# Turning the q and k rows of a second attention layer: DVE blocks and SBUF transfers in place of TensorE transpositions

## What is computed

```python
q = rmsnorm((x @ Wq + bq).reshape(b, n, 32, 128), gq)
k = rmsnorm((x @ Wk + bk).reshape(b, n, 32, 128), gk)
v = (x @ Wv + bv).reshape(b, n, 32, 128)
attn = softmax(einsum("bnhd,bmhd->bhnm", q, k) / sqrt(128))
out = einsum("bhnm,bmhd->bnhd", attn, v).reshape(b, n, 4096) @ Wo + bo
```

## Time and profile before

| | us |
|---|---|
| median of the runs shown | 2192.4 |
| span of the profiled execution | 2194.5 |
| PE busy in it | 2089.6 (95%) |
| DVE busy | 1678.1 (76%) |
| ACT busy | 1349.4 (61%) |
| POOL busy | 1216.8 (55%) |

### The profile page before, as it was taken

The page is one execution under the profiler, slowest core; times in us unless marked ns, Lnnn a source line. Parts: engine busy times, 40 slices in busy tenths (PEclk is TensorE's granted clock), DMA queues, the critical chain, the costliest instruction groups (busy, mean ns, idle before and its releaser), DMA issues. The chain is left out here.

```text
span 2194.5 us, 37916 instructions
## 1 busy us (share of the span) xinstructions
PE 2089.6 (95%) x10535; PEld 1756.7 (80%) x10535; DVE 1678.1 (76%) x2972; ACT 1349.4 (61%) x3637; POOL 1216.8 (55%) x985
## 2 busy tenths in 40 slices
PE   6999999999999778999999999999999999878998
PEld 4788888888888657888888888888888888756786
DVE  6788888888888876878888788888878888875422
ACT  5877777777776455656666565666656565544321
POOL 3878777787786554546454554545445463354300
PEclk9999999999999989999999999999999999979999
DMA  2534344434344422444444444434444343533210
GB/s 83 136 100 126 108 110 113 114 105 125 104 117 130 134 62 71 116 108 116 116 109 99 121 107 115 109 100 117 114 112 112 99 116 92 131 104 105 87 53 25
DMA packets 165887, 231.69 MB, mean 106 GB/s; under 512 B 47280, under 2 KB 77136, under 8 KB 165744
## 3 DMA queue, kind: packets, MB, share of 16 engines
q1 hardware_dynamic: 165744, 229.97, 39.4%
HBM read 114.23 MB, written 6.55 MB: 55 GB/s over the span
## 5 line engine op out<-in xcount | busy, mean ns | idle before, releaser
L90 POOL TENSOR_TENSOR l_probsT_lo<-l_moved,l_probsT_hi 128x512 fp32r<-128x512 f32 (+2 forms) x256 | 278.1, 1091 | 291.9 <-ACT l_probsT_hi L946 264.5
L940 ACT ACTIVATE l_probs<-l_score,l_negtop 128x512 f32<-128x512 f32 x256 | 176.1, 688 | 354.3 <-DVE l_negtop L1051 342.3
L90 DVE TENSOR_TENSOR l_probsT_lo<-l_moved,l_probsT_hi 128x512 fp32r<-128x512 f32 (+1 forms) x256 | 285.9, 1117 | 33.4 <-ACT l_probsT_hi L946 33.4
L1831 ACT ACTIVATE l_probs<-l_score,l_negtop 128x128 f32<-128x128 f32 (+3 forms) x256 | 135.0, 527 | 170.4 <-DVE l_negtop L1944 169.6
L1051 DVE TENSOR_REDUCE l_negtop<-l_score 128x1 f32<-128x512 f32 x256 | 175.5, 686 | 74.9 <-PE l_score L85 72.6
L83 PE MATMUL l_score<-l_kT_lo,l_qT_hi 128*128 128x512 f32 (+3 forms) x512 | 190.4, 372 | 24.1 <-POOL l_qT_lo L90 9.4
L83 PE MATMUL l_out<-l_w_out_lo,l_oT_hi 128*128 128x512 f32 x512 | 209.2, 409 | 2.8 <-DVE l_oT_lo L90 2.6
L84 PE MATMUL l_out<-l_w_out_hi,l_oT_lo 128*128 128x512 f32 x512 | 201.8, 394 | 0.0
L85 PE MATMUL l_out<-l_w_out_hi,l_oT_hi 128*128 128x512 f32 x512 | 201.5, 394 | 0.0
L83 PE MATMUL l_general<-l_w_qk_lo,xT_hi 128*128 128x512 f32 x504 | 198.1, 393 | 2.5 <-PEq L1451 2.5
L1944 DVE CUSTOM_DVE_ANT_0 l_score<-l_score,l_mask 128x128 f32<-128x128 f32 (+3 forms) x256 | 126.1, 493 | 96.9 <-PE l_score L85 95.5
(11 more groups left out here) (249 smaller groups left out, 6283.4 us busy)
## 6 DMA issues: line engine op xcount, KB each, us to landing
l_moved<-l_blocks SPq DMA_DIRECT2D x1024, 64.0 KB, 2.0
l_moved<-l_blocks SPq DMA_DIRECT2D x512, 80.0 KB, 2.1
l_inv_all<-inv_rows SPq DMA_DIRECT2D x32, 512.0 KB, 4.2
l_raw_out<-l_wo SPq DMA_DIRECT2D x64, 256.0 KB, 4.2
l_inv_all<-inv_rows SPq DMA_DIRECT2D x64, 256.0 KB, 3.6
l_raw_q<-l_wq SPq DMA_DIRECT2D x32, 256.0 KB, 4.1
l_raw_qk<-l_wq SPq DMA_DIRECT2D x64, 128.0 KB, 2.9
l_raw_qk<-l_wk SPq DMA_DIRECT2D x64, 128.0 KB, 3.0
```

Source lines behind the costliest of these rows:

```text
L90: return engine.tensor_tensor(out, full, hi.bitcast(F32), ALU.subtract)
L940: act.activation(probs[:, n % NPR], score[n % 2][:], ACT.Exp, bias=negtop[:, n:n + 1], accum_out=total[:, n:n + 1]).then_inc(s_exp, 1)
L1831: act.activation(probs[:, n % NPR, 0:width[t]], score[n % 2][:, 0:width[t]], ACT.Exp, bias=negtop[:, n:n + 1], scale=-1.0, accum_out=total ...
```

## The change

The first two slots of the whole layer still use PE (`turn_first`). For the other 31 pairs:

- PE's `tq` and `tk` uses are gone.
- DVE transposes each normalised `y` tile in 32x32 blocks into a new buffer `y_blocks` (`TURNS1`, steps -6, -6, -5, -5 of the pair, at the end of DVE's step).
- SP issues 16 transfers per pair from `y_blocks` back into `y` (`MOVES1`, step -5, ahead of `move` in the queue's order). The source of each is 2 KB per partition; the destination is four runs of 512 B in each of 32 partitions.
- ACT makes the upper halves from `y` in SBUF (`HALVES1`, q at -3 and k at -2 of each slot, after the exponential and ahead of `landed_hi`), and for k also scales `y` in place.
- POOL makes the lower halves (`rows_lo`), after its `landed_lo`.
- The tokens inside q and k are then in another order, so the score product reads its keys in runs of 32, and DVE's reading of the `pv` bank changes its order.
- The bias rows `b_qk` have one buffer in place of two; they are loaded at -17 behind a wait for the last `y` of the previous half group. Some semaphores of other stages are merged.

In places of the cycle: row turns on DVE at 2 and 3, row transfers on SP at 3, upper halves on ACT at 5 and 6 (first slot of the pair) and 1 and 2 (second slot).

```diff
-USES1 |= {(kind, s): 4 * s + n for kind, n in (("tq", -4), ("tk", -3), ("pv", PV_AT)) for s in range(SLOTS)}
+USES1 |= {("pv", s): 4 * s + PV_AT for s in range(SLOTS)}
+TURNS1 = Plan({(r, b, t): 16 * r + 8 * b - 6 + t // 2 for r, b in PAIRS for t in range(TB)}, lambda x: x)
+MOVES1 = Plan({(r, b): 16 * r + 8 * b - 5 for r, b in PAIRS})
+HALVES1 = Plan({(kind, s): 4 * s + n for kind, n in (("q", -3), ("k", -2)) for s in range(SLOTS)})
-BIAS1 = Plan({(r,): 16 * r - 22 for r in range(2)})
+BIAS1 = Plan({(r,): 16 * r - 17 for r in range(2)})
...
+            def move_rows(m, unit, d):
+                b = unit[1]
+                sp.wait_ge(s_y_block, m.done(TURNS1, (*unit, TB - 1), d) - TB)
+                sp.nop(nofuse=True)
+                for g in range(TB):
+                    for c in range(C):
+                        sp.dma_start(y[32 * c:32 * c + 32, b, :, g * P:(g + 1) * P],
+                                     y_blocks[32 * g:32 * g + 32, c]).then_inc(s_y_move, 16)
...
+                    for x, d in m.turns(MOVES1, n):
+                        move_rows(m, x, d)
                     slot = m.slot_at(n, MOVE_AT)
                     if slot is not None:
                         move(m, slot)
...
-                    for t in range(TB):
-                        last = pe.transpose(bank[:, t * P:(t + 1) * P], y[:, b, t, at:at + HD], ident[:])
...
-                            pe.wait_ge(s_free, m.done(USES1, ("tk", slot)))
+                            pe.wait_ge(s_qk_lo, m.done(HALVES1, ("k", slot)))
...
-                        product(nc, score[n % 2][:], qT[:, slot % 2, t * P:(t + 1) * P], kT[:, slot % 2])\
+                        keys = Split(by_tile(kT.hi[:, slot % 2]), by_tile(kT.lo[:, slot % 2]))
+                        product(nc, tokens(score[n % 2][:]), qT[:, slot % 2, t * P:(t + 1) * P], keys)\
...
+            def rows_hi(x, m, d):
+                kind, s = x
+                r, b, _ = pair_of(s)
+                act.wait_ge(s_y_move, y_moved(m, (r, b), d))
+                if kind == "q":
+                    last = act.activation(qT.hi[:, s % 2], item_of(x), ACT.Copy)
                 else:
+                    act.activation(kT.hi[:, s % 2], item_of(x), ACT.Copy, scale=gains[:, 2:3])
+                    last = act.activation(item_of(x), item_of(x), ACT.Copy, scale=gains[:, 2:3])
+                last.then_inc(s_qk_hi, 1)
...
+                    for x, d in m.turns(HALVES1, n):
+                        if not by_hand(m, d, x[1]):
+                            rows_hi(x, m, d)
                     for slot, k in landing(m, n):
                         landed_hi(m, slot, k)
...
+            def turn_rows(m, x, d):
+                r, b, t = x
+                if t == 0:
+                    n = m.number(MOVES1, (r, b), d) - 2
+                    if not (m.first and n <= 0):
+                        dve.wait_ge(s_y_move, m.i * (MOVES * len(PAIRS)) + MOVES * n)
+                        dve.nop(nofuse=True)
+                dve.wait_ge(s_yn, m.done(USES1, ("y", r, b, t), d, of_y))
+                to = y_blocks.rearrange("p c n x -> p n c x")[:, :, :, 32 * t:32 * t + 32]
+                dve.transpose(to, y[:, b, t]).then_inc(s_y_block, 1)
...
+            def rows_lo(x, m, d):
+                kind, s = x
+                pool.wait_ge(s_qk_hi, m.done(HALVES1, x, d))
+                to = (qT if kind == "q" else kT)[:, s % 2]
+                rest(pool, to.lo, item_of(x), to.hi).then_inc(s_qk_lo, 1)
```

More of the change, by code:

```diff
@@ L599, in load_bias @@
     def load_bias(self, sp):
-        for r in range(2):
-            for e in range(2):
-                rows = self.a[("l1_bq", "l1_bk")[e]][0:1, r * 2 * HD:(r + 1) * 2 * HD]
-                sp.dma_start(self.b_qk[:, r, e * 2 * HD:(e + 1) * 2 * HD], rows.to_broadcast([P, 2 * HD]))\
-                    .then_inc(self.s_b[r], 16)
+        for e in range(2):
+            rows = self.a[("l1_bq", "l1_bk")[e]][0:1, 0:2 * HD]
+            sp.dma_start(self.b_qk[:, e * 2 * HD:(e + 1) * 2 * HD], rows.to_broadcast([P, 2 * HD]))\
+                .then_inc(self.s_b, 16)
         for k, n in enumerate(("l1_gq", "l1_gk")):
@@ L731, in bank_of, with first_turned, by_hand, item_of @@
             return general[(m.number(USES1, x, d) - 1) % len(general)]
+        def first_turned(h, kind):
+            return (score, out_bank)[h][kind == "k"]
+        def by_hand(m, d, slot):
+            return m.first and d == 0 and slot < 2
+        def item_of(x):
+            r, b, h = pair_of(x[1])
+            return y[:, b, h + 2 * (x[0] == "k")]
+        def by_tile(rows):
+            return rows.rearrange("p (g t i) -> p t g i", g=TB, t=TB)
+        def y_moved(m, unit, d):
+            return MOVES * m.number(MOVES1, unit, d) + m.i * (MOVES * len(PAIRS)) - MOVES
         def landing(m, n):
@@ L862, in bank_use, with turn_first @@
                 last.then_inc(s_bank, 1)
+            def turn_first(h):
+                for kind in QK:
+                    at = (h + 2 * (kind == "k")) * HD
+                    for t in range(TB):
+                        to = first_turned(h, kind)[:].rearrange("p (g t i) -> p t g i", g=TB, t=TB)[:, t]
+                        last = pe.transpose(to, y[:, 0, t, at:at + HD], ident[:])
+                    last.then_inc(s_first, 1)
             for x in USES1.early[TB:]:
+                if x[3] == TB - 1:
+                    pe.wait_ge(s_yn, TB)
+                    turn_first(0)
                 bank_use(x, start, 0)
+            turn_first(1)
             def project(m, x, d):
@@ L958, in output_hi @@
                 act.activation(oT.hi[:, s % 2], scaled[:], ACT.Identity, bias=b_v[:, h:h + 1]).then_inc(s_o_hi, 1)
-            for k, x in enumerate(USES1.early):
-                if of_halved(x):
+            for x in LOADS1.early[C:]:
+                work(x, start, 0)
+            for x in USES1.early[TB:]:
+                if x[3] == 2:
                     act.wait_ge(s_zero, 1)
-                    bank_hi(x, start, 0)
-                elif k in (TB, TB + 1):
-                    square(x, start, 0)
-                if k == TB - 1:
-                    for x in LOADS1.early[C:]:
-                        work(x, start, 0)
-            for t in range(2, TB):
-                square(("y", 0, 1, t), start, 0)
+                    first_hi(0)
+                square(x, start, 0)
+            first_hi(1)
             def body(m):
@@ L1004, in bank_use @@
                         dve.nop(nofuse=True)
-                        dve.wait_ge(s_b[r], (m.i + d + 1) * 32)
-                    if t == 0 and m is not start and not (m.first and d == 0 and r == 0):
+                        dve.wait_ge(s_b, (m.i + d) * 64 + 32 * (r + 1))
+                    if m is not start and not (m.first and d == 0 and r == 0):
                         dve.nop(nofuse=True)
-                        dve.wait_ge(s_bank, m.done(USES1, ("tk", pair_slots(1 - r, b)[1]), d - (r == 0)))
-                    last = dve.tensor_tensor(y[:, b, t], bank[:], b_qk[:, r], ALU.add)
+                        read = ("q", "k")[t // 2], pair_slots(1 - r, b)[t % 2]
+                        dve.wait_ge(s_qk_lo, m.done(HALVES1, read, d - (r == 0)))
+                    last = dve.tensor_tensor(y[:, b, t], bank[:], b_qk[:], ALU.add)
                 elif kind == "v":
@@ L1021, in bank_use @@
                     wait_past(dve, s_inv_dma, m, 32 * SLOTS, 32 * (slot + 1))
-                    last = dve.tensor_tensor(tokens(scaled[:]), by_token(bank[:]), inv_all[:, slot % 2].rearrange("p (g i t) -> p t g i", g=TB, t=TB), ALU.mult)
+                    last = dve.tensor_tensor(tokens(scaled[:]), tokens(bank[:]), inv_all[:, slot % 2].rearrange("p (t i g) -> p t g i", g=TB, t=TB), ALU.mult)
                 last.then_inc(s_free, 1)
@@ L1107, in body @@
                         add_rows(m, x, d)
+                    for x, d in m.turns(TURNS1, n):
+                        turn_rows(m, x, d)
                     if n in (10, 26):
@@ L1148, in body @@
                             landed_lo(m, slot, k)
+                    for x, d in m.turns(HALVES1, n):
+                        if not by_hand(m, d, x[1]):
+                            rows_lo(x, m, d)
                     for x, d in m.turns(USES1, n, 2):
```

129 lines of the change are left out of this document (65 added, 64 removed).

## The result

The kernel after takes 2464.52 us (median of 4 runs, 2461.66 to 2468.98), the kernel before on the same chip 2195.45 (2192.38 to 2200.07). The ratio is 1.1226 [1.121, 1.1243], so the change costs 12%. The profiled execution of the kernel after has a span of 2459.8 us. The forecast was 2415, the range 2295 to 2500.

A forecast was written before the change was run, and what follows sets the result against it. PE was taken to bound the kernel. Per cycle, 34.8 us less 1.8 for turns, plus 7.5 pause and 1.5 clock, gave 42.0; +7.2, over 31 pairs +223 on 2192.4, made 2415 us, range 2295 to 2500.

The forecast's parts named there:

- The mechanism: Row turns, 16 SP issues, landing, ACT's and POOL's halves run late; PE pauses 7.5 us per cycle at `pv`, place 6.
- S: Zero point of the forecast's times within a cycle, in us: the start of PE's score of place 4.
- The unknown price: One issue of the new row transfers on SP: taken at 0.626 us start to start, bounds 0.333 and 0.795, landing 2.0.
- rivals 1: SP's row issues are dearer because runs are four times as many, 0.795 us each: 2511 us, chance 0.12.
- 2 (0.333): Rival: SP's row issues are cheap, 0.333 us each, pause 3.6 us: 2248 to 2295 us, chance 0.10.
- SP's order: Row transfers precede place 4's `move` in SP's queue, so turned probabilities start 10 us later, hidden behind the first wait.
- Reading the keys in runs of 32: PE's score product reading keys in runs of 32 words: taken as nothing; at half speed 5.5 us per cycle.
- The merged semaphores and the bias step: Semaphores gathering transfers waited for at nearly the same places, and bias loading at -17: both taken to cost nothing.
- Mis-sized: the clock: PE's passes run slower after the pause because the granted clock falls: 1.5 us added per cycle.
- Mis-sized: the waits: PE standing still for chunk 2's lower half at `pv` in place 6: 7.5 us, once per cycle.
- These three: Added work on DVE, ACT and POOL, hidden by PE's work; without that cover 0, 1.3 and 5.2 us per cycle.
- rival 4: Transfers land in time, PE stays the bound and its turns are simply gone: 2137 us, chance 0.04.

The follow-up runs named there:

- e2: Kernel after with only 8 of the 16 row transfers per pair issued, half of q and k rows left old: 2287.58 us, ratio 1.0418.
- e7: Kernel after with the 16 transfers replaced by 4 writes to DRAM and 4 reads back, issued by SP, turns at -7: 2336.52 us, ratio 1.0642.
- e1: Kernel after with ACT taking the landed probabilities ahead of the q and k halves from the moved rows: 2436.58 us, ratio 1.1104.
- e5: Kernel after without the row transfers, ACT waiting for DVE's turns instead, q and k from unmoved rows: 2206.57 us, ratio 1.0045.
- e3: Kernel after with 27 unneeded PE passes put ahead of the pause in place 6, output unchanged: 2450.68 us, ratio 1.1169.
- e13: e5 with POOL's lower and ACT's upper q and k halves a quarter wide, ACT's scaling of k left out: 2173.47 us, ratio 0.9905.

## Why the prediction was right, and where its terms were off

- **The mechanism held, step by step.** DVE's turns end at S + 2.1 (forecast 2.2), the rows are landed at S + 14.3 (13.9), the lower half is ready at S + 16.8 (16.4), PE wants it at S + 9.0 (8.9). The pause stands where it was put, once per pair, with the waits named. e2 with e7 shows that the issues set it; e1 that it isn't tied to `pv`.
- **The unknown price** came out next to the nearest row: 0.601 us for one issue against 0.591 of the probabilities', landing 2.0. From start to start it is 0.65 where 0.626 stood (20 sets of 16 take 10.34 us in the median). The four runs of 512 B at the destination cost nothing to speak of. So rivals 1 (0.795) and 2 (0.333) both fell. On the landing the Trainium skill's rule (DMA: Bandwidth & Descriptors, Why small descriptors are slow) was borne out: no penalty between SBUF and SBUF, 2.0 us. The Trainium skill's other rule, that large descriptors are what matters when the issuing queue is solid (Perfetto Trace Analysis, What "DMA-bound" means), wasn't: a quarter of the piece size changed the issue by 0.01 us, and what mattered was the number of issues.
- **SP's order.** The probabilities moved in place 4 do come 10 us later. The last of their issues starts at 1520.2 and has landed at 1522.5, S + 25.5 as forecast, and ACT takes them at 1527.0. So the delay is hidden, as forecast. ACT does stand still for 2.6 us just before it takes them, and PE 0.74 a step later for `v_lo`, but the view puts ACT's 2.6 down to "issue", which means that it shows nothing that ACT waited for. It has five such gaps, 12 us in all.
- **Reading the keys in runs of 32** cost next to nothing: score passes start 0.231 us apart before and 0.234 after, 0.1 us for the 24 of a cycle. The merged semaphores and the bias step show no wait of their own.
- **Mis-sized: the clock.** 1.5 us per cycle were added, from the earlier trace rows; measured are 2.2. After a pause of 7.7 us the slow passes reach into place 7, up to 1518.7: not seven passes but nine of 512 columns and some three of 256. That is 0.7 x 31 = 22 us.
- **Mis-sized: the waits.** PE's idle time is 8.0 us per pair, with the starts 8.2, where 7.5 stood: 0.7 x 31 = 22 us. Some pauses are longer (up to 8.5), and small waits for `v_lo`, for one value weight and for exponentials come on top. The longer spacing of the issues has 15 x 0.023 = 0.35 of the 0.7. Together clock and waits are 44 of the 49 us by which 2415 fell short. Of the rest 3 are the kernel before, which took 2195.45 us beside this run and 2192.4 in the forecast.
- **Wrong, though it didn't show: what hides the added work.** "These three are hidden by PE's work" and rival 4's 2137 both assumed that PE's turns are all gain once the transfers are in time. e5 gives 2207, not 2137 to 2141. The prediction asked how idle ACT and POOL are over a stretch, 36 and 48%, and not how late each is at the places where PE takes something from it. By the earlier trace rows chunk 2's lower half was ready at 1410.93 and wanted at 1412.13; that slack is 1.2 us, and the two turns ahead of it, 0.9, were most of it. That the slow clock hides waits, as e3 shows, belongs here as well: the terms of the sum were added as if each stood alone.

## What to carry to other kernels

Work taken off the full engine is won only as far as its suppliers have slack at the very instruction that waits for them. Read that slack (ready time against wanted time) at each hand-over, not the idle share of a stretch, and take off it whatever the change puts ahead on each supplier. Count a queue that is not in the busy table, such as the one that issues transfers, like an engine: issues times price, plus its waits, against the cycle. And where transfers replace computation, the number of issues was the price here; another order at the consumer only moved the wait, and bigger pieces through DRAM traded issues for a second landing.

## What the runs showed of the hardware

- One issue of 64 KB between 32 and 32 partitions of SBUF takes 0.601 us with 512 B pieces at the destination and 0.590 with 2 KB pieces in the same kernel; writes of 256 KB from 32 partitions to DRAM take 0.634 (median of 124), reads back 0.421. Four times the bytes per issue cost 5% more in the one case and less in the other, though one end is DRAM there.
- The granted clock falls within a pause of 7.7 us and after pauses of 2.3 to 2.7 (e2), and it can be kept at 1.00 by passes that nobody needs (e3); but the time didn't follow, since other waits came up (14 us of 68).
- POOL's lower half of q takes 1.73 us (mean of 62), the same operation for k 1.29 (mean of 62). Operands and sizes are alike. The timelines show that POOL and DVE hold each other up when both read a lower half's two operands from SBUF. DVE's half of a chunk, begun while POOL's is running, ends 0.55 us after POOL's in each of 52 cases (0.54 to 0.56, kernel after). POOL's q half is the next one, begun while DVE's is running, and ends 1.15 us after DVE's. With a quarter of the width (e13) it takes 0.92 us where it begins beside DVE's half (47 cases) and 0.46 where it doesn't (9 cases), and that of k takes 0.46. So the 0.45 us is waiting and not work, twice per pair on the chain to the keys.
